# Router steps of the mixture-of-experts stage moved one place earlier on VectorE

## What is computed

```python
x = x + attn(layernorm(x), ...)      # 32 query heads, 8 key heads of 16, softmax over 512 keys, plus a memory read
h = layernorm(x)
scores = sigmoid(h @ router_w.T)                     # 16 experts
_, topk_idx = top_k(scores + e_bias, 4)
topk_w = take(scores, topk_idx); topk_w /= topk_w.sum(-1) + 1e-20
x = x + sum over chosen experts e of topk_w[e] * down_e(silu(gate_e(h)) * up_e(h)) + shared_expert(h)
```

## Time and profile before

| | us |
|---|---|
| median of 3 runs | 1856.76 |
| lowest and highest | 1853.92, 1857.07 |
| profiled execution | 1851.41 |
| its span, first to last instruction | 1849.4 |

### The profile page before, as it was taken

One profiled execution on the slowest core, in us unless ns is written; L12 is line 12 of the kernel. 1 busy time (PEld: TensorE's weight loads), 2 busy tenths in 40 slices (PEclk: granted clock), 3 DMA queues, 4 the chain that ended last, 5 costly groups with the idle time before them and its releaser, 6 DMA issues.

```text
span 1849.4 us, 35292 instructions
## 1 busy us (share of the span) xinstructions
PE 1765.4 (95%) x8536; PEld 899.7 (49%) x8537; DVE 1144.6 (62%) x2172; ACT 883.9 (48%) x1756; POOL 920.6 (50%) x1127
## 2 busy tenths in 40 slices
PE   6899999999999999999999898999999999999995
PEld 5444445455455545554433354545555555555542
DVE  5667787878888888878788646333334433334333
ACT  2367777776777777777777641221222112221210
POOL 3533557676677666676635555033333343333441
PEclk9899999999999999999999999999999999999998
DMA  6423325344534444343344489698888988888889
GB/s 198 123 70 65 90 83 154 102 112 136 157 94 111 137 125 111 117 144 102 101 126 161 154 299 351 181 200 163 161 155 159 167 162 160 154 162 167 161 179 254
DMA packets 255898, 277.76 MB, mean 150 GB/s; under 512 B 57888, under 2 KB 184096, under 8 KB 253024
## 3 DMA queue, kind: packets, MB, share of 16 engines
q0 software_dynamic: 40880, 106.96, 27.4%
q1 hardware_dynamic: 151600, 127.10, 25.2%
q10 hardware_dynamic: 63296, 42.24, 8.2%
HBM read 145.65 MB, written 135.74 MB: 152 GB/s over the span
## 4 chain that ended last, share of the span: by engine, by line
PE 80%; DVE 5%; DMA 5%; ACT 3%; issue 2%; POOL 2%; SPq 1%; ACTq 0%; DVEq 0%; POOLq 0%
PE ps_gu L1986 22%; PE ps_pv L1255 12%; PE ps_exp L1226 10%; PE ps_max L1212 9%; PE ps_y L2003 7%; PE ps_misc L1133 5%; PE ps_y L2013 4%; DVE mx L1002 3%; DMA wts_sb<-second_sum_rows 2%; PE ps_misc L1104 2%; ACT prob L739 2%; PE ps_misc L1144 1%; PE ps_misc L1269 1%; PE ps_misc L1181 1%; PE ps_misc L1120 1%
## 5 line engine op out<-in xcount | busy, mean ns | idle before, releaser
L1002 DVE TENSOR_REDUCE mx<-ps_max 128x2 f32<-128x1024 f32 x512 | 621.4, 1220 | 151.1 <-PE ps_max L1212 131.0
L739 ACT ACTIVATE prob<-ps_exp 128x512 f32<-128x512 f32 x992 | 569.1, 597 | 147.3 <-PE ps_exp L1226 127.2
L1986 PE MATMUL ps_gu<-wts_sb,xT 128*128 x1152 | 399.3, 490 | 1.1 <-POOLq L1644 0.8
L1226 PE MATMUL ps_exp<-qs,ks 98*128 98x512 bf16 x992 | 378.3, 382 | 13.9 <-ACT prob L739 12.6
L1212 PE MATMUL ps_max<-ks,qs 96*128 96x512 bf16 x1024 | 306.4, 380 | 7.3 <-DVE mx L1002 5.3
L1737 ACT ACTIVATE gs<-ps_gu 128x192 f32<-128x192 f32 x176 | 58.3, 331 | 520.7 <-PE ps_gu L1986 322.6
L1685 POOL DMA_INDIRECT out<-yt,idx x72 | 111.7, 1551 | 365.4 <-ACT yt L1747 281.9
L1986 PEld LDWEIGHTS ps_gu<-wts_sb,xT 128*128 128x128 f32 x1152 | 209.7, 190 | 161.3 <-issue 45.9
L1255 PE MATMUL ps_pv<-prob,vs 128*32 128x512 f32 x2048 | 251.5, 604 | 0.2 <-ACT prob L747 0.2
L1226 PEld LDWEIGHTS ps_exp<-qs,ks 98*128 98x128 bf16 x992 | 96.6, 97 | 176.5 <-ACT prob L739 62.0
L1895 DVE SCALAR_TENSOR_TENSOR hid<-ps_gu,wsel,gs 128x192 f32<-128x192 f32 (+2 forms) x216 | 68.4, 344 | 177.3 <-ACT gs L1737 177.3
(11 more groups left out here) (197 smaller groups left out, 2016.5 us busy)
## 6 DMA issues: line engine op xcount, KB each, us to landing
xt<-rows_by_expert SPq DMA_DIRECT2D x296, 64.0 KB
dnr_sb<-in_dnr SPq DMA_DIRECT2D x144, 128.0 KB
xt<-rows_by_expert ACTq DMA_DIRECT2D x280, 64.0 KB
qk_parts<-parts POOLq DMA_DIRECT2D x112, 120.0 KB, 3.6
qs<-qk_parts SPq DMA_DIRECT2D x64, 192.0 KB, 3.0
wts_sb<-in_wts ACTq DMA_DIRECT2D x12, 1024.0 KB, 9.1
x_sb<-in_x SPq DMA_DIRECT2D x16, 512.0 KB, 4.5
qs<-qk_parts SPq DMA_DIRECT2D x64, 128.0 KB, 3.1
```

The lines of the kernel that those rows point to most:

```text
L739: act.activation(prob[:, s, q], ps_exp[:, q % 2], ACT.Exp, scale=SCALE).then_inc(s_exp, 1)
L1002: dve.tensor_reduce(mx[:, k % 2, 4 * s + 2 * p:4 * s + 2 * p + 2], ps_max[:, p], AX_X, ALU.max).then_inc(s_maxd, 1)
L1226: pe.matmul(ps_exp[:, q % 2], ks[0:ROWS + MROWS, kk, s * P:(s + 1) * P], qs[0:ROWS + MROWS, kk, q], start=True, stop=True).then_inc(s_sc, 1)
L1986: mm = pe.matmul(ps_gu[:, i, 0:2 * I], xT[:, i, d], w, start=(d == 0), stop=(d == DC - 1))
```

## The change

The steps `router`, `best` and `chosen` of units 0 to 12 move from places 12, 13 and 14 to places 11, 12 and 13. The tables of the other engines read other entries (`T`, `logits`, `rank`, `slots`, `scatter`), which stay. Units 13, 14 and 15 stay.

```diff
     LAST = {"residual": -10, "stats": (-4, 0), "norm": 0, "T": (4, 8), "logits": 9, "router": 12, "best": 13,
             "chosen": 14, "rank": 17, "weights": 19, "slots": 23, "scatter": 24}
-    USUAL = LAST | {"rank": 16}
+    USUAL = LAST | {"router": 11, "best": 12, "chosen": 13, "rank": 16}
```

## The result

The changed kernel is slower: 1865.8 us (median of 4 runs, 1865.25 to 1870.99) against 1855.34 (4 runs, 1851.66 to 1857.07), a ratio of 1.0061 with a 95% interval from 1.0046 to 1.0075. Measured once more it was 1861.85 against 1852.95, 1.0051 (1.0037 to 1.0064). The forecast was 1866.7, +9.9 us; the two ratios give +11.3 and +9.4 us (the medians lie 10.5 and 8.9 us apart).

A forecast was written before the change was run, and what follows sets the result against it. The prediction took TensorE, busy 95% of the span, to bound the kernel, VectorE counting only where TensorE waits for it. 7.8 + 0 + 2.06 = 9.9 us on 1856.76 gave 1866.7 us, range 1859.5 to 1871.0.

The forecast's parts named there:

- Router in its new place: VectorE, units 0 to 9: input ready, L943 takes 0.18 us, L945 ends with L532, maximum 12 starts at 581.79.
- The three slots: TensorE, units 0 to 9: place 14 no wait, place 15 0.35 us late, place 16 0.78 in all; together 7.8 us.
- One sign: In the profile after the change, TensorE's total wait on L1002 should rise by about 9 us.
- Unit 10: L945 gets in before GpSimd's L546, so TensorE does not wait: 0 us, with 0.73 as the upper end.
- Units 11 and 12: No projection unit beside them: place 16 starts 1.03 us late, its old wait mostly moves to place 15; 2.06 us together.
- The sum: Whole kernel: 7.8 + 0 + 2.06 = 9.9 us, all on the path, put on the median of 1856.76.
- Rank: TensorE's rank matmul: its input `mkb` is 0.9 us early already, so bringing it sooner gives 0.
- A: Rival: TensorE wins its lateness back in idle time later in each round; +2.8 us, 1859.6 us; chance 0.14.
- B: Rival, units 0 to 9: L945 misses the gap after L532, place 16 2.01 us late; +22.2, 1878.9 us; chance 0.07.
- C: Rival, units 0 to 9: L945 escapes L532 and VectorE's lead removes TensorE idle time; -5.0, 1851.8 us; chance 0.05.

The follow-up runs named there:

- the changed order without stops: The changed kernel with two GpSimd tensor_tensor operations, L532 and L546, replaced by copies of 16 columns; 1.0021 (1.0009 to 1.0033) of the kernel before.
- the run one place further: `router`, `best` and `chosen` at places 10, 11 and 12, one place sooner than the change; 1.0034 (1.0021 to 1.0047) of the kernel before.

## Why the prediction was right

*Router in its new place:* the input was there, as said. L943 took 0.44 us where 0.18 was taken. It ends at 583.00, 0.04 after L462, a tensor_scalar: GpSimd's tensor_scalar holds it too. L945 was reached later for that, at 583.65, and still ended with L532, at 1.20 us where 1.45 was named. Maximum 12 starts 2.43 us after L943, as against 2.42. The sizes of the two parts were off and the sum was right, and that is not luck: L945 ends 0.05 us after L532 in all ten units, whenever it is reached, and the prediction had said that up to 0.5 us for L943 would change nothing.

*The three slots:* place 14 no wait, as said; place 15 +0.36 (0.35 predicted), place 16 +0.77 in all (0.78). Ten units cost 0.78 each by the rounds. Router, best and chosen alone and together show the steps one by one: 0, +0.38, +0.78, and chosen alone +0.88 where 0.87 was expected. One sign came out smaller than named: TensorE's waits on L1002 rose from 3.2 to 10.1 us in all, 6.9 and not about 9, because the idle times in brackets count less than a wait costs, as said above; for the same reason the brackets of places 15 and 16 show 0.18 and 0.25 where 0.35 and 0.43 were named.

*Unit 10:* no wait, as taken: L945 took 0.19 us, L546 started at its usual distance, and from place 14 to place 18 it takes 8.36 us before and after. By the rule of the Trainium skill ("SBUF — State Buffer", section "SBUF: two separate sides") L943, which has two SBUF inputs, should also be held by L462, as by any GpSimd operation that reads SBUF. In unit 5 it was; the rule was the better guide there than my reading of the rows. The other half of the rule, which the prediction leaned on, that a VectorE step which starts first holds GpSimd up, no run here shows: L546 took its 1.27 us in unit 10 although it began 0.11 us before L945 ended. So unit 10 came out at 0, but not by a hold that a row shows. Timelines of the two engines there, in the changed kernel:

```profile
905.49 0.19 DVE L945 SCALAR_TENSOR_TENSOR rt<-rt,eb_sb 128x32 f32<-128x32 f32 x1
```
```profile
905.57 1.27 POOL L546 TENSOR_TENSOR sig<-sig,sg 128x512 f32<-128x512 f32 x1 [3.69 <-ACT sig L707]
```

*Units 11 and 12:* +1.02 in unit 11 (1.03 predicted). The old wait did not move into place 15, as the prediction put it in words: TensorE waits at both places now, 1.04 and 1.12 us by the brackets where it was 1.09 at place 16 alone. The prediction's own times, 961.05 and 963.22, imply this. Unit 12 lost 2.59 where 1.03 was predicted. **This term was mis-sized by 1.6 us**: the waits came as forecast, but the granted clock of TensorE fell behind them, which no step of the prediction had, though the fall did not come in unit 11, with the same waits. Stretches of the changed kernel: places 14 to 18 in units 11 and 12, then 3.5 us within the latter.

```profile
966.10:975.06 8.96, 6.47 (x39) 1.74 (x38) 7.23 (x17) 4.99 (x10) 0.00 (x0) 1.00 0.22 55
1022.06:1032.58 10.52, 8.02 (x38) 1.80 (x37) 7.34 (x17) 4.99 (x10) 0.00 (x0) 0.84 0.19 47
```
```profile
1027.50:1031.00 3.50, 3.50 (x21) 0.41 (x13) 1.98 (x6) 0.52 (x1) 0.00 (x0) 0.51 0.29 58
```

*The sum:* 10 x 0.78 + 0 + 1.02 + 2.59 = 11.4 us by the trace, 9.9 predicted, +11.3 and +9.4 measured. That the median of 1865.8 lies only 0.9 us below the forecast of 1866.7 is partly luck: the kernel before came out at 1855.34 and not at the 1856.76 that the forecast started from, and this offsets the missing term of the clock. *Rank:* nothing was gained, as said. A slip that changes nothing: the profile shows 12 instructions of VectorE moved per unit, not 13.

*The rivals.* A (given back within the round): the rounds are longer by the full 0.78. B (L945 misses the gap): it got through in all ten units, ending 0.05 us after L532 each time. C (L945 escapes): not in the changed kernel; where it was made to, the loss went but no gain came, since TensorE had no wait to lose.

One number needs a remark: the profiled execution of the changed kernel took 1870.99 us, 5 above its median, and its span is 19.6 us longer than the one before. Of that 8.6 us lie behind place 18 of unit 12, where nothing was changed: 836.4 us from there to the end, against 827.8 before. The second profiled execution of the same kernel, with a span of 1858.0, takes 825.8 there, less than the one before, so the 8.6 us can't be put down to the change. What makes them isn't worked out. The longest wait of TensorE where the experts begin is 6.2 us long:

```profile
1185.60 5.48 PE L1986 MATMUL ps_gu<-wts_sb,xT 128*128 x8 [6.17 <-POOLq L1644]
```

It does not explain them by itself: the execution before and the second one of the changed kernel have a wait of 6.6 and 6.2 us on L1986 there too.

## What to carry to other kernels

When steps move on an engine that feeds a double-buffered hand-over, list for each slot how long it is free before the other engine wants it, and price each moved step by what it puts ahead of the slot with the least lead: here the lightest step, put ahead of a slot with a lead of 0.21 us, cost by itself as much as the whole change, while the heaviest, put ahead of one with 2.54, cost nothing. A short step can be long in its new place if another engine holds what it needs; look up what runs beside it there. Such a sum, made from rows of one round and multiplied, came within 2 us of 11; what it lacked was the clock.

## What was not expected of the hardware

TensorE's granted clock fell to its lower level, 1.2 of 2.4 GHz, after the longest waits of these rounds. In the traces with over 2 us of waiting at places 14 to 16 of units 11 and 12 (the changed kernel twice, the change for units 10 to 12 twice, the changed order without stops, `chosen` alone: 12 such units) it fell in 7. In the 16 such units of the other eight traces it fell in none: 14 of them have at most 1.2 us of waiting, and the two of the run one place further 1.8 us, in waits of 0.55, 1.12 and 0.09 us at places 14 to 16. The fall lasted 3.4 us in six of these and cost 1.3 to 1.6 us; in unit 11 of the changed order without stops it lasted 6.8 us, and the P times V matmuls and what follows took 2.4 us longer than in its unit 12. Each trace is of one execution, so how often it falls in the others is not known, and why it falls in one unit and not in the next with the same waits isn't settled.
